# Feed-forward attention: the query side's band moves from four matmuls into VectorE's row maxima

## The chip, the cores and the metric

The kernel runs on one core of one Trainium2 chip. The metric is the time on the device in microseconds (us), the median of a few runs.

## The reference, cut to what matters

The program computes an adaptive-layernorm block: two attentions of 16 heads over four sequences of 1024 rows of 128, and then two layers of a feed-forward block that has a local attention of its own. The change touches that local attention alone:

```python
DIM_HEAD, WINDOW, HEADS = 64, 64, 8        # DEPTH = 2 layers
bq = q.reshape(b, h, w, WINDOW, d) * QK_SCALE          # 8.0
sim = jnp.einsum('bhwid,bhwjd->bhwij', bq, bk)         # keys: this window and the one before
mask = (i < j) | (i > j + WINDOW) | (j == -1)
sim = jnp.where(mask, -jnp.finfo(sim.dtype).max, sim)
attn = jax.nn.softmax(sim, axis=-1)
out = jnp.einsum('bhwij,bhwjd->bhwid', attn, bv)
```

A query at place i sees the keys from i - 64 to i. That is the band.

## The kernel before, in words

Rows are worked on in tiles of 128. The feed-forward half is one stream of 64 tiles (2 layers x 4 sequences x 8 tiles; `STREAM`), written as a software pipeline in `ffn_stream`: in period n each engine does some steps of tile n, some of n - 1, n - 2 and n - 3, in an order written out by hand in one loop for each engine. An engine runs its list strictly in order; semaphores hold an instruction until its operands are there. Besides, after every four tiles a chunk of 512 rows goes through the MLP (`CHUNK_TILES = 4`), and its steps are spread over the following periods by `step`, 0 to 3. So the pattern repeats every four periods. In this text the four are called A (step 0: `gate`, three `down` matmul pairs, `add_residual`, `finish`), B (step 1: `x_transposes`, `row_stats`), C (step 2: `normalise_rows`, first `up_gelu`) and D (step 3: the other `up_gelu`, three Gelus with two table loads).

The scores are computed twice. First on the query side, rows are queries: `query_scores(n)` (lines 1351 to 1371) makes q k^T in bf16 for 8 heads in two PSUM banks, 128 x 1024. From it comes the row maximum of every query and head (`row_maxima`, L1810), negated and in bf16. That is transposed (`max_transpose`, L1375), copied by ScalarE (`copy_max`, L1639) and added by small matmuls (L1393) to the second scores, `key_scores(n)` (L1387 to L1402), in which rows are keys. Their exponentials (L1646) feed `value_products` (L1416). A key outside a query's band must not enter its maximum, so the query side starts with four matmuls (L1359): a 64 x 64 corner of the bf16 identity times a band of 0 and -1e30, widened over four heads, written with `start=True`; the 16 score matmuls (L1367) are then added to it with `start=False`. The four corners (`CORNERS`) are the 64-row halves of both operands and of the output. The key side has a band of its own, L1387, which the change leaves alone.

For the first tile of a sequence there is no window before: `form = 1` is a band that hides the first 64 keys of queries 0 to 63, and their score matmuls write the upper 64 columns alone (`lo`).

TensorE's order in period n, around the change: project_qk(n) (L1327), project_v(n) (L1337), key_scores(n-2), qk_transposes(n-1) (L1347), value_products(n-2) (L1416), **query_scores(n-1)** (L1359, L1367), project_out(n-3) (L1438), MLP steps (L1463, L1448), out_transposes(n-2) (L1424), `down` in A (L1489), **max_transpose(n-1)** (L1375). That last one waits for `maxed`.

VectorE's order: normalise_rows in C (L1852), normalise_heads(n-1) (L1270), rope(n) (L1785, L1788), square_sums(n) (L1802, L1804), `gate` j=1 in A, norm_out(n-2) (L1819, L1824), `gate` j=2 in A (L1861), **row_maxima(n-1)** (L1810), gate j=0 in D, add_residual in A (L1836), row_stats in B (L1843, L1846), `finish` in A (L1869). norm_out waits for value_products; row_maxima waits for query_scores.

In the first six periods leftovers of the attention half (`tail_...`) run between these steps.

Of the kernel before, what the change touches and what calls it, by code (L numbers as in the profile page):

```python
# [23 lines left out]
BF16 = mybir.dt.bfloat16  # L24
ALU = mybir.AluOpType
ACT = mybir.ActivationFunctionType
AX = mybir.AxisListType.X

P = 128
B, S, D = 4, 1024, 128  # L30
TILES = S // P
BANK = 512
# [21 lines left out]
DEPTH, FH, FD = 2, 8, 64  # L54
INNER = FH * FD
WIN = 64
# [4 lines left out]
HIDDEN = -1e30  # L61
# [3 lines left out]
SIDES = 2  # L65
SIDE_HEADS = FH // SIDES
# [25 lines left out]
class Scope:  # L92
# [12 lines left out]
    def sb(self, name, shape, dtype=F32):  # L105
        return self.stack.enter_context(self.nc.sbuf_tensor(f"{self.prefix}_{name}", shape, dtype))
# [9 lines left out]
def widen(ap, shape):  # L116

    return ap.to_broadcast(shape)
# [1117 lines left out]
def ffn_stream(nc, psum, dram, keep, k, tail):  # L1236


    g = k.signals
    bank = lambda i, n=1: psum[:, i * BANK:(i + n) * BANK]  # L1240
    QK_BANK, V_BANK, SCORE_BANK, MAX_BANK, KEY_BANK, OT_BANK, WO_BANK, MLP_BANK = 0, 2, 2, 3, 4, 4, 6, 7
    UP_BANKS = {(0, 0): 7, (1, 0): 1, (2, 0): 0, (0, 1): 7, (1, 1): 7, (2, 1): 1}
    SIDE_ROWS = (slice(0, FD), slice(FD, P))
    CORNERS = ((0, 0), (1, 0), (0, 1), (1, 1))
# [12 lines left out]
    near, pick = stage[:, 0:P], stage[:, P:P + SIDE_HEADS * FD].rearrange("p (h c) -> p h c", h=SIDE_HEADS)  # L1257
# [14 lines left out]
    with nc.Block() as block:  # L1272
# [34 lines left out]
        def _(pe):  # L1307
            T = nc.tensor
# [42 lines left out]
            def query_scores(n):  # L1351
                t = n % TILES
                pe.wait_ge(g["qkt_copied"], n + 1)
                if n == 0:
                    pe.wait_ge(g["bands_ready"], 1)
                for side, block_n in CORNERS:
                    rows, c0 = SIDE_ROWS[side], (SCORE_BANK + side) * BANK
                    form = 1 if t == 0 and block_n == 0 else 0
                    T.matmul(psum[SIDE_ROWS[block_n], c0:c0 + BANK], keep.ident_bf[rows, rows],  # L1359
                             widen(k.band_bf[rows, form:form + 1, :], [FD, SIDE_HEADS, P]),  # L1360
                             start=True, stop=True)
                for i in range(SIDE_HEADS):
                    for side, block_n in CORNERS:
                        rows, q0 = SIDE_ROWS[side], t * P + block_n * WIN
                        lo = WIN if t == 0 and block_n == 0 else 0
                        c0 = (SCORE_BANK + side) * BANK + i * P
                        ins = T.matmul(psum[SIDE_ROWS[block_n], c0 + lo:c0 + P],  # L1367
                                       k.q_t_bf[rows, i, q0:q0 + WIN, 1],
                                       k.k_t_bf[rows, i, q0 - WIN + lo:q0 + WIN, 1],
                                       start=False, stop=True, skip_group_check=True)  # L1370
                ins.then_inc(g["s_in_psum"], 1)

            def max_transpose(n):
# [168 lines left out]
            for n in range(PERIODS):  # L1542
                c, step = divmod(n - 6, CHUNK_TILES)
# [180 lines left out]
        def _(pool):  # L1724
            steps = Chain(pool, g["pool_steps"])
            halves = lambda ap: ap.rearrange("p (h i d) -> p h i d", h=2 * FH, i=2)
            cleared = g["cleared"]
# [2 lines left out]
            pool.memset(k.max_t[:], 0.0).then_inc(cleared, 1)  # L1730
            pool.memset(k.neg_max[:], 0.0).then_inc(cleared, 1)
            pool.memset(k.xw[:, :, 0:1], 0.0).then_inc(cleared, 1)
            pool.memset(k.band_bf[:, 1, 0:WIN], HIDDEN).then_inc(cleared, 1)
            pool.memset(k.band_t_bf[:, 2, 0:WIN], HIDDEN).then_inc(cleared, 1)
            pool.memset(k.v_back[:], 0.0).then_inc(cleared, 1)
            gated_add(pool, steps, tail, keep, 2, g["tail_gated"])
# [31 lines left out]
        def _(dve):  # L1768
            steps = Chain(dve, g["dve_steps"])
            V = nc.vector  # L1770
# [35 lines left out]
            def row_maxima(n):  # L1806
                dve.wait_ge(g["s_in_psum"], n + 1)
                if n >= 2:
                    dve.wait_ge(g["mt_in_psum"], n - 1)
                steps.did(V.tensor_reduce(k.neg_max[:, n % 2, :].rearrange("p (s c) -> p s c", s=SIDES)[:, :, 0:SIDE_HEADS],  # L1810
                                          bank(SCORE_BANK, 2).rearrange("p (s i c) -> p s i c", s=SIDES, i=SIDE_HEADS),
                                          AX, ALU.max, negate=True), g["maxed"])

            def norm_out(n):
                dve.wait_ge(g["o_in_psum"], n + 1)
# [58 lines left out]
            def make_bands():  # L1874
                dve.wait_ge(g["loaded"], FIRST_LOADS)
                steps.did(V.tensor_copy(k.band_bf[:, 0, :], near))
                steps.did(V.tensor_copy(k.band_bf[:, 1, WIN:P], near[:, WIN:P]))
                steps.did(V.tensor_copy(k.band_t_bf[:, 0, :], near))
                steps.did(V.tensor_copy(k.band_t_bf[:, 1, 0:WIN], near[:, WIN:P]))
                steps.did(V.tensor_copy(k.band_t_bf[:, 1, WIN:P], near[:, 0:WIN]))  # L1880
                steps.did(V.tensor_copy(k.band_t_bf[:, 2, WIN:P], near[:, 0:WIN]))
                steps.did(V.tensor_copy(k.pick[:], pick), g["bands_ready"])
# [88 lines left out]
def ffn_half(nc, psum, dram, keep, tail):  # L1971
    with Scope(nc, "ffn", keep.stack) as k:
        sb = k.sb
# [17 lines left out]
        k.k_t_bf = k.k_t.bitcast(BF16).rearrange("p i (t w) -> p i t w", w=2)  # L1991
        k.v, k.v_back = sb("v", [P, RING, VF_COLS]), sb("v_back", [P, RING, VF_COLS])
        k.band_bf, k.band_t_bf = sb("band", [P, 2, P], BF16), sb("band_t", [P, 3, P], BF16)
        k.pick = sb("pick", [P, SIDE_HEADS, FD], BF16)
        k.neg_max, k.max_t = sb("neg_max", [P, 2, P], BF16), sb("max_t", [P, 2, P], BF16)
        k.probs = sb("probs", [P, 2, SIDES, SIDE_HEADS, P])
# [113 lines left out]
```

## Time and profile before

| what | value |
|---|---|
| median of 3 runs | 1262.74 us (1262.25 to 1264.91) |
| the profiled execution's own time | 1263.66 us |
| span in its profile | 1261.9 us |
| TensorE matmul busy | 1141.8 us, 90% |
| VectorE busy | 987.2 us, 78% |
| ScalarE busy | 830.2 us, 66% |
| GpSimd busy | 444.9 us, 35% |
| L1359, the query side's band | 256 matmuls of 64 x 512, 400 ns each |
| L1367, the query side's scores | 1024 matmuls, median 215 ns |
| L1810, the row maxima | 64 reductions of 128 x 1024, 77.6 us, 1213 ns each |

The feed-forward half begins at about 523 us. Matmuls are pipelined, and matmuls on different corners of the array run side by side, so durations of TensorE rows may not be added: what a group costs is read from when the next one starts. The same holds, by less, for VectorE: a row's duration reaches a little past the start of the next row.

### The profile page before, as it was taken

How to read it: one execution, taken by the hardware profiler on the slowest of the kernel's cores; microseconds unless marked ns; L12 is line 12 of the kernel's file. 1: busy time of each engine (PE TensorE's matmuls, PEld its weight loads, DVE VectorE, ACT ScalarE, POOL GpSimd, SP SyncE). 2: the span in 40 equal slices, each digit the busy share in tenths (PEclk: the TensorE clock that was granted, in tenths of full speed). 3: DMA queues.
4: the chain of work that ended last, by engine and by line, in shares of the span. 5: the costliest groups of instructions: out<-in, count | busy, mean ns of one | idle time of the engine just before them, and what ended most of it. 6: DMA issues, size and time to landing. Idle time of an engine off the chain costs nothing.

```text
span 1261.9 us, 36707 instructions
## 1 busy us (share of the span) xinstructions
PE 1141.8 (90%) x15602; PEld 693.7 (55%) x15602; DVE 987.2 (78%) x1556; ACT 830.2 (66%) x1229; POOL 444.9 (35%) x582
## 2 busy tenths in 40 slices
PE   4488889898989999778999999999999999999985
PEld 3133434344435655455666666676666666666662
DVE  7869685877768888896887887788778877887755
ACT  3498898989887867545556655665666566656541
POOL 2203221211206448855533433333333333333310
PEclk8599999999999989998999999999999999999997
DMA  3114120020213331100210110111111111111102
GB/s 106 34 25 137 50 91 35 18 101 18 69 51 135 119 134 69 50 18 20 82 24 22 30 30 16 26 30 24 24 27 23 28 23 27 28 23 28 27 6 67
DMA packets 37329, 59.78 MB, mean 47 GB/s; under 512 B 6416, under 2 KB 12464, under 8 KB 37168
## 3 DMA queue, kind: packets, MB, share of 16 engines
q1 hardware_dynamic: 35760, 56.61, 15.3%
q8 instruction: 124, 2.03, 0.7%
q10 hardware_dynamic: 1408, 0.84, 0.3%
q14 instruction: 37, 0.30, 0.1%
HBM read 22.58 MB, written 16.78 MB: 31 GB/s over the span
## 4 chain that ended last, share of the span: by engine, by line
PE 51%; DVE 4%; ACT 2%; issue 1%; DVEq 0%; ACTq 0%
PE psum L1327 9%; PE psum L1463 7%; PE psum L1416 6%; PE psum L1438 5%; PE psum L1402 5%; PE psum L1337 4%; PE psum L1347 4%; PE psum L1489 3%; PE psum L1424 2%; PE psum L1387 2%; PE psum L1359 2%; ACT ffn_probs L1646 2%; PE psum L1393 1%; PE psum L1367 1%; PE psum L1455 1%
## 5 line engine op out<-in xcount | busy, mean ns | idle before, releaser
L818 ACT ACTIVATE att_probs<-psum 128x1024 f32<-128x1024 f32 (+2 forms) x384 | 350.7, 988 | 44.5 <-PE psum L673 44.3
L1757 POOL TENSOR_TENSOR ffn_rot<-ffn_rot,ffn_rot_sin 128x512 f32<-128x512 f32 x128 | 160.2, 1273 | 372.5 <-DVE ffn_rot L1788 372.5
L717 PE MATMUL psum<-att_probs,att_v 128*32 128x256 f32 (+3 forms) x3712 | 201.4, 343 | 6.5 <-DVE att_probs L1010 3.2
L673 PE MATMUL psum<-att_q_stack,att_k_parts 64*128 64x512 bf16 (+4 forms) x1280 | 142.1, 296 | 41.8 <-ACT att_probs L818 30.4
L717 PEld LDWEIGHTS psum<-att_probs,att_v 128*32 128x32 f32 x3712 | 96.1, 110 | 72.0 <-issue 41.8
L1010 DVE TENSOR_TENSOR att_probs<-att_probs,att_causal_mask 128x1024 f32<-128x1024 f32 (+1 forms) x80 | 95.9, 1214 | 35.3 <-ACT att_probs L818 35.2
L673 PEld LDWEIGHTS psum<-att_q_stack,att_k_parts 64*128 64x128 bf16 x1280 | 43.5, 94 | 144.5 <-ACT att_probs L818 104.0
L1639 ACT ACTIVATE ffn_max_t<-psum 68x128 bf16<-68x128 bf16 x64 | 17.5, 273 | 156.8 <-PE psum L1375 156.7
L1646 ACT ACTIVATE ffn_probs<-psum 128x1024 f32<-128x1024 f32 x64 | 65.6, 1025 | 59.1 <-PE psum L1402 59.1
L1608 ACT ACTIVATE ffn_sq<-psum 128x512 f32<-128x512 f32 x128 | 74.7, 595 | 22.0 <-PE psum L1327 21.1
L604 POOL TENSOR_TENSOR att_rot<-att_qk 128x1280 f32<-128x1280 f32 x6 | 16.5, 2756 | 204.9 <-ACT att_qk L849 204.9
L1416 PEld LDWEIGHTS psum<-ffn_v_back,ffn_probs 128*64 128x64 f32 x1024 | 64.5, 137 | 31.8 <-ACT ffn_probs L1646 18.0
L585 POOL TENSOR_TENSOR att_probs<-att_probs,att_local_mask 128x480 f32<-128x480 f32 (+1 forms) x48 | 64.8, 1360 | 42.6 <-ACT att_probs L818 42.3
L1810 DVE TENSOR_REDUCE ffn_neg_max<-psum 128x8 bf16<-128x1024 f32 x64 | 77.6, 1213 | 0.0
L1802 DVE TENSOR_REDUCE ffn_ssq_floor<-ffn_sq 128x16 f32<-128x1024 f32 x64 | 77.3, 1208 | 0.0
L1416 PE MATMUL psum<-ffn_v_back,ffn_probs 128*64 128x65 f32 x1024 | 73.4, 224 | 2.1
L1270 DVE TENSOR_TENSOR ffn_rot<-ffn_rot,ffn_rnorm 128x704 f32<-128x704 f32 x64 | 68.9, 1077 | 7.9 <-POOL ffn_rnorm L129 7.3
L1347 PE MATMUL psum<-ident,ffn_rot 128*128 128x128 f32 x512 | 70.8, 282 | 3.3 <-DVE ffn_rot L1270 3.3
L1416 PE MATMUL psum<-ffn_v,ffn_probs 128*64 128x65 f32 x1024 | 73.4, 224 | 0.0
L1631 ACT ACTIVATE ffn_qk_t<-psum 128x1024 f32<-128x1024 f32 x64 | 65.6, 1025 | 10.4 <-PE psum L1347 10.4
L1402 PE MATMUL psum<-ffn_qk_t 64*64 64x64 f32 (+1 forms) x2944 | 70.1, 236 | 0.0
L1327 PE MATMUL psum<-tail_f_wqkv,xs 128*128 128x512 f32 x128 | 65.5, 637 | 3.2 <-PEq L539 1.8
(222 smaller groups left out, 2443.1 us busy)
## 6 DMA issues: line engine op xcount, KB each, us to landing
ffn_v_back<-ffn_v SPq DMA_DIRECT2D x120, 130.0 KB, 2.4
att_q_stack<-q_rows SPq DMA_DIRECT2D x28, 512.0 KB, 3.6
q_rows<-att_q_high SPq DMA_DIRECT2D x21, 256.0 KB, 4.5
q_rows<-att_q_mid SPq DMA_DIRECT2D x21, 256.0 KB, 4.2
q_rows<-att_q_low SPq DMA_DIRECT2D x14, 256.0 KB, 4.0
xres<-in_hidden SPq DMA_DIRECT2D x4, 512.0 KB, 6.1
out<-ffn_qk_t SPq DMA_DIRECT2D x3, 512.0 KB, 3.2
tail_f_wqkv<-in_f_wqkv SPq DMA_DIRECT2D x1, 768.0 KB, 4.5
```

Source lines behind the costliest of these rows:

```text
L673: ins = T.matmul(psum[:, banks[i] + at:banks[i] + at + width], k_parts[rows, p % 3, j, kt * P:(kt + 1) * P], q_stack[rows, turn % 2, j, q0 ...
L717: ins = T.matmul(psum[32 * g:32 * g + V_PAD, (4 + cc) * BANK + lo - cc * BANK: (4 + cc) * BANK + hi - cc * BANK], v[:, p % 4, kt, g, shift ...
L818: act.activation(probs[:, n % E_BUFS, 2 * j:2 * j + 2, 0:width], ps2((step % 2) * 2).rearrange("p (h c) -> p h c", h=2)[:, :, 0:width], AC ...
L1010: c.did(V.tensor_tensor(blocks, blocks, widen(seen, list(blocks.shape)), ALU.mult), masked)
L1327: T.matmul(bank(QK_BANK + i), keep.xs[:, b, t * P:(t + 1) * P], k.w_qkv[layer][:, i * INNER:(i + 1) * INNER], start=True, stop=True).then_ ...
L1347: ins = T.transpose(psum[:, SCORE_BANK * BANK + i * P:SCORE_BANK * BANK + (i + 1) * P], k.rot[:, n % 2, i * P:(i + 1) * P], keep.ident[:])
L1402: ins = T.matmul(psum[SIDE_ROWS[key_block % 2], c0 + lo:c0 + hi], k.k_t[rows, i, key_block * WIN:(key_block + 1) * WIN], k.q_t[rows, i, t ...
L1416: ins = T.matmul(psum[SIDE_ROWS[block_n], c0:c0 + VF], k.probs[:, n % 2, side, i, block_n * WIN:(block_n + 1) * WIN], values[:, n % RING, ...
L1463: T.matmul(psum[0:rows, UP_BANKS[j, part] * BANK:(UP_BANKS[j, part] + 1) * BANK], k.w1[layer][:, lo:lo + rows], k.hn[:], start=True, stop= ...
L1646: steps.did(act.activation(k.probs[:, n % 2].rearrange("p s i c -> p (s i c)"), bank(KEY_BANK, 2), ACT.Exp, scale=QK_SCALE), g["exped"])
L1757: steps.did(pool.tensor_tensor(out, out, halves(k.rot_sin[:, n % 2, :])[:, :, 1 - half, :], ALU.add), g["added"] if half else None)
L1810: steps.did(V.tensor_reduce(k.neg_max[:, n % 2, :].rearrange("p (s c) -> p s c", s=SIDES)[:, :, 0:SIDE_HEADS], bank(SCORE_BANK, 2).rearran ...
```

## The change

The four band matmuls go. The 16 score matmuls are written with `start=True`, and so hold plain scores. In place of one reduction over 8 heads VectorE runs, for each head, one fused operation: (scores + band) x -1 in bf16 to a new scratch tensor, and the minimum of it, from a start of 2e30, into that head's column of `neg_max`. The band is read from SBUF in bf16, now with all 128 query rows at once, so its second form is made for 128 rows too: the memset covers rows 0 to 63 and a cast more fills rows 64 to 127. The column of head i of side s is `64 s + i`, as before.

```diff
@@ query_scores(n), TensorE
-                for side, block_n in CORNERS:
-                    rows, c0 = SIDE_ROWS[side], (SCORE_BANK + side) * BANK
-                    form = 1 if t == 0 and block_n == 0 else 0
-                    T.matmul(psum[SIDE_ROWS[block_n], c0:c0 + BANK], keep.ident_bf[rows, rows],
-                             widen(k.band_bf[rows, form:form + 1, :], [FD, SIDE_HEADS, P]),
-                             start=True, stop=True)
...
-                                       start=False, stop=True, skip_group_check=True)
+                                       start=True, stop=True, skip_group_check=True)
@@ GpSimd, once
-            pool.memset(k.band_bf[:, 1, 0:WIN], HIDDEN).then_inc(cleared, 1)
+            pool.memset(k.band_bf[0:WIN, 1, 0:WIN], HIDDEN).then_inc(cleared, 1)
@@ row_maxima(n), VectorE
-                steps.did(V.tensor_reduce(k.neg_max[:, n % 2, :].rearrange("p (s c) -> p s c", s=SIDES)[:, :, 0:SIDE_HEADS],
-                                          bank(SCORE_BANK, 2).rearrange("p (s i c) -> p s i c", s=SIDES, i=SIDE_HEADS),
-                                          AX, ALU.max, negate=True), g["maxed"])
+                form = 0 if n % TILES else 1
+                for side in range(SIDES):
+                    for i in range(SIDE_HEADS):
+                        c0, column = (SCORE_BANK + side) * BANK + i * P, side * FD + i
+                        steps.did(V.tensor_tensor_reduce(k.hidden_scores[:, SIDE_HEADS * side + i], psum[:, c0:c0 + P], k.band_bf[:, form, :], -1.0,
+                                                         -2 * HIDDEN, ALU.add, ALU.min,
+                                                         k.neg_max[:, n % 2, column:column + 1]),
+                                  g["maxed"] if (side, i) == (SIDES - 1, SIDE_HEADS - 1) else None)
@@ make_bands(), VectorE, once
                 steps.did(V.tensor_copy(k.band_bf[:, 1, WIN:P], near[:, WIN:P]))
+                steps.did(V.tensor_copy(k.band_bf[WIN:P, 1, 0:WIN], near[WIN:P, 0:WIN]))
@@ ffn_half
+        k.hidden_scores = sb("hidden_scores", [P, FH, P], BF16)
```

What the diff does not show is what one call of `tensor_tensor_reduce` becomes in VectorE's queue. Here is that queue at a tile of kind B, before (`ffn_o` is the normalised attention output, `ffn_neg_max` the negated maxima, `ffn_stats` the MLP's row statistics):

```order
L1802 TENSOR_REDUCE ffn_ssq_floor<-ffn_sq 128x16 [waits ffn_rn_ready,ffn_sq_ready]
L1804 TENSOR_REDUCE ffn_ssq<-ffn_ssq_floor 128x16 [waits ffn_dve_steps]
L1819 RECIPROCAL ffn_o_rec<-psum 128x8 [waits ffn_o_in_psum]
L1824 TENSOR_TENSOR ffn_o<-psum,ffn_o_rec 128x2x4x64 [waits ffn_ot_in_psum,ffn_dve_steps]
L1810 TENSOR_REDUCE ffn_neg_max<-psum 128x2x4 [waits ffn_mt_in_psum,ffn_s_in_psum]
L1843 BN_STATS ffn_stats<-psum 128x6 [waits ffn_xt_in_psum]
```

And the head of the same place in the changed kernel, where the maxima have line 1808; the last two rows below come eight times in all, ahead of the row statistics:

```order
L1818 RECIPROCAL ffn_o_rec<-psum 128x8 [waits ffn_o_in_psum]
L1823 TENSOR_TENSOR ffn_o<-psum,ffn_o_rec 128x2x4x64 [waits ffn_ot_in_psum,ffn_dve_steps]
L1808 ISA ffn_hidden_scores,ffn_neg_max<-psum,ffn_band 128x128 [waits ffn_mt_in_psum,ffn_s_in_psum]
L1808 ISA ffn_neg_max 128x1
L1808 ISA ffn_hidden_scores,ffn_neg_max<-psum,ffn_band 128x128
L1808 ISA ffn_neg_max 128x1
```

Each call is two instructions: one over 128 x 128, and one of a single column that reads the running minimum out into `neg_max`. One instruction of 1024 columns has become sixteen, eight of 128 columns and eight of one. What stands ahead of them and behind them, and all waits, are the same. On TensorE the four rows of L1359 are gone and nothing has moved; the queues of ScalarE, GpSimd and SyncE hold the same instructions in the same order as before.

## Rows read from the trace of the kernel before

**Rows 1.** Busy time by stretch, feed-forward; the last columns are granted clock and DMA.

```profile
core 0: us, PE busy (x) PEld busy (x) DVE busy (x) ACT busy (x) POOL busy (x), PEclk, DMA share, GB/s
...
560.00:600.00 40.00, 33.29 (x473) 22.85 (x473) 29.13 (x57) 22.91 (x42) 24.25 (x28) 0.91 0.11 25
...
899.70:942.06 42.36, 42.25 (x616) 28.06 (x614) 34.12 (x52) 25.73 (x44) 16.20 (x28) 1.00 0.12 27
```

**Rows 2.** Timeline, VectorE: start us, us, engine, line, operation; the maxima of four tiles.

```profile
899.70 1.21 DVE L1810 TENSOR_REDUCE ffn_neg_max<-psum 128x8 bf16<-128x1024 f32 x1
...
909.38 1.21 DVE L1810 TENSOR_REDUCE ffn_neg_max<-psum 128x8 bf16<-128x1024 f32 x1
...
919.05 1.22 DVE L1810 TENSOR_REDUCE ffn_neg_max<-psum 128x8 bf16<-128x1024 f32 x1
...
929.62 1.22 DVE L1810 TENSOR_REDUCE ffn_neg_max<-psum 128x8 bf16<-128x1024 f32 x1
...
942.06 1.21 DVE L1810 TENSOR_REDUCE ffn_neg_max<-psum 128x8 bf16<-128x1024 f32 x1
```

**Rows 3.** Timeline, TensorE: the transposes of the maxima that follow them.

```profile
901.85 0.22 PE L1375 MATMUL psum<-ident_bf,ffn_neg_max 128*68 128x128 bf16 x1
...
910.85 0.22 PE L1375 MATMUL psum<-ident_bf,ffn_neg_max 128*68 128x128 bf16 x1
...
920.53 0.22 PE L1375 MATMUL psum<-ident_bf,ffn_neg_max 128*68 128x128 bf16 x1
...
931.52 0.22 PE L1375 MATMUL psum<-ident_bf,ffn_neg_max 128*68 128x128 bf16 x1
```

**Rows 4.** Timeline, TensorE: the band, the scores and what follows, one tile.

```profile
908.41 0.41 PE L1359 MATMUL psum<-ffn_band,ident_bf 64*64 64x512 bf16 x4
908.65 0.40 PE L1367 MATMUL psum<-ffn_qk_t 64*64 64x128 bf16 x16
908.98 1.16 PE L1438 MATMUL psum<-ffn_o_t,tail_space 128*128 128x128 f32 x8
```

**Rows 5.** Timeline, VectorE: from the maxima of A to those of B.

```profile
900.83 1.39 DVE L1836 TENSOR_TENSOR ffn_xw<-xs,psum 64x512 f32<-64x512 f32 x2
...
904.74 1.23 DVE L1785 TENSOR_TENSOR ffn_rot_sin<-psum,tail_space 128x1024 f32<-128x1024 f32 x1
...
908.53 0.21 DVE L1819 RECIPROCAL ffn_o_rec<-psum 128x8 f32<-128x8 f32 x1
908.77 0.69 DVE L1824 TENSOR_TENSOR ffn_o<-psum,ffn_o_rec 128x512 f32<-128x512 f32 x1
```

**Rows 6.** Timeline, VectorE: behind the maxima of B.

```profile
910.61 0.89 DVE L1843 BATCH_NORM_STATS2 ffn_stats<-psum 128x6 f32<-128x128 f32 x4
911.53 0.38 DVE L1846 BATCH_NORM_AGGREGATE ffn_mv<-ffn_stats 128x2 f32<-128x6 f32 x4
912.52 1.37 DVE L1852 TENSOR_SCALAR ffn_xn<-psum,ffn_mv,ffn_rstd 128x128 f32<-128x128 f32 x4 [0.60 <-ACT ffn_rstd L1661]
```

**Rows 7.** One line each, VectorE: duration ns min/median/max.

```profile
L1843 DVE BATCH_NORM_STATS2 ffn_stats<-psum x64: 278/281/300, 612.3 to 1235.1; 128x6 f32<-128x128 f32 x64
...
L1846 DVE BATCH_NORM_AGGREGATE ffn_mv<-ffn_stats x64: 147/151/184, 613.2 to 1235.7; 128x2 f32<-128x6 f32 x64
```

**Rows 8.** Timeline, VectorE: where it waits for TensorE, C to D and D to A.

```profile
928.77 0.21 DVE L1819 RECIPROCAL ffn_o_rec<-psum 128x8 f32<-128x8 f32 x1 [1.89 <-PE psum L1416]
...
941.39 0.75 DVE L1861 SCALAR_TENSOR_TENSOR tail_space<-psum,ffn_b,tail_space 85x512 f32<-85x512 f32 x1 [1.58 <-PE psum L1463]
```

**Rows 9.** Timeline: maxima that TensorE waited for, and the weight load behind them.

```profile
552.26 1.21 DVE L1810 TENSOR_REDUCE ffn_neg_max<-psum 128x8 bf16<-128x1024 f32 x1
...
553.53 0.11 PEld L1375 LDWEIGHTS psum<-ident_bf,ffn_neg_max 128*68 128x68 bf16 x1 [0.71 <-DVE ffn_neg_max L1810]
```

**Rows 10.** VectorE by line and form: two casts of the bands, the slowest and the fastest.

```profile
L1880 DVE CAST ffn_band_t<-ffn_probs 128x64 bf16<-128x64 f32 x1 | 1.3, 1289 | 0.0
...
L1877 DVE CAST ffn_band<-ffn_probs 128x64 bf16<-128x64 f32 x1 | 0.2, 202 | 0.0
```

## The prediction

> **What bounds the kernel now.** I read the busy time by stretch first. Over four tiles of the feed-forward stream, 42.36 us, TensorE's rows cover 42.25 us and VectorE's 34.12 us, at a granted clock of 1.00, its 2.4 GHz level [rows 1]. TensorE's cover says little, since its rows overlap; what counts is when each step starts. So next the timeline of the row maxima and of the transposes behind them. The maxima of the four tiles A, B, C, D start at 899.70, 909.38, 919.05 and 929.62, and the next A's at 942.06: distances of 9.68, 9.67, 10.57 and 12.44 us [rows 2]. These four numbers come back within 0.1 us from the start at 645.71 to the last A at 1196.05, so one round stands for all.
>
> Then, for each distance, what sets it. From A to B VectorE runs from one instruction into the next: none of its rows in that stretch shows idle time, and norm_out at 908.53 and 908.77 leads straight into B's maxima [rows 2, 5]. From B to C it idles 0.60 us, for ScalarE's two roots, which wait for its own row statistics [rows 6]; that gap moves along with the maxima. From C to D it waits 1.89 us for the value products, and from D to A 1.58 us for the MLP matmul ahead of gate L1861 [rows 8]: there TensorE sets the pace. The maxima are on TensorE's path as well: their transpose (L1375) is the last thing that it does in a period, and nothing of the next period can pass it. It starts 2.15 us after the start of A's maxima, 1.47 after B's, 1.48 after C's and 1.90 after D's [rows 2, 3]. A reduction takes 1.21 us, and where TensorE did wait for one, its weight load came 0.06 us after the end [rows 9]. So in B and C the transpose has some 0.2 us to spare, in D 0.6, in A 0.9.
>
> **What goes.** The next group starts 0.24 us after the four band matmuls do (908.41 to 908.65), though each row's duration is longer [rows 4]. So TensorE gets 0.24 us back per tile, 15 us over 64 tiles if nothing else held. It does not get it in A to B and B to C, where VectorE sets the distance. It gets it once ahead of L1861, and it brings D's transpose forward from 1.90 to 1.66.
>
> **What comes.** One reduction holds VectorE 1.13 us (899.70 to 900.83) and ends at 1.21 [rows 2, 5]. In its place stand sixteen instructions. No row shows a fused operation or a read-out of its result, so I bound a head by neighbours. Four statistics of 128 columns from PSUM take 0.89 us together, one of them 0.281: the next starts (0.89 - 0.281) / 3 = 0.203 us after the one before. Four aggregates of six columns take 0.38, one 0.151: a start every 0.076 us [rows 6, 7].
> - Low end, 0.203 us a head: the read-out is hidden behind the next head.
> - A start every 0.203 + 0.076 = **0.279** us a head. I take this: the two rows are instructions of the same engine, the same width and the same source, back to back without a wait, as the new ones are.
> - The read-out starts when the head's duration is over: 0.281 + 0.076 = 0.357.
> - High end, neither overlaps anything: 0.281 + 0.151 = 0.432.
>
> With 0.279 VectorE is held X = 8 x 0.279 = 2.23 us, and the last result is there at Z = X + 0.075 = 2.31, a read-out's duration reaching that far past its slot.
>
> The rows show that short independent instructions overlap. The Trainium skill, "VectorE: DVE Perf Modes", section "The DRAIN you can't avoid", says that the next operation cannot issue until the pipe is empty, and its rules for kernel authors say to minimise the count of operations; by that the high end would hold, 1397 us, a rival below. The same page, in "Two Vector instructions with no wait between them", counts an accumulator output as a second instruction that is held only for what it reads and where it writes; by that the read-out here is not held, and the value is the one that I take.
>
> **The sum, per round of four tiles.**
> - A to B, VectorE sets it: 2.23 - 1.13 = +1.10. TensorE's way would be Z + 0.10 to the transpose (0.06 from [rows 9] and up to some hundredths for the load), and 7.53 from there (901.85 to 909.38): 9.94, less than 9.68 + 1.10.
> - B to C, the same: +1.10. TensorE's way is 2.41 + 8.20 = 10.61 against 10.77.
> - C to D, TensorE sets it: the transpose comes at 2.41 in place of 1.48, and the 9.09 us from there to D's maxima stay: +0.93.
> - D to A: 2.41 in place of 1.90, less the band's 0.24 ahead of L1861: +0.27.
>
> That is **+3.40 us** a round; for a price d of a head it is 32 d - 5.53. Between the maxima at 602.23 and the last at 1214.60 lie 58 distances, 14.5 rounds: +49.3. The six tiles before are filled with leftovers of the attention half that stand in VectorE's queue behind the maxima: 6 x 1.10 = +6.6. The cast more in make_bands costs 0.2, and at worst 1.3 [rows 10]. The smaller memset and the scratch tensor cost nothing: they lie in GpSimd's idle time before the first scores and in free memory. The queues of ScalarE, GpSimd and SyncE hold what they held; their work moves with the tiles. Behind the longer maxima VectorE's queue holds A's residual, B's statistics, D's gate and then normalise_heads, for which TensorE's L1347 waits. VectorE's 8.2 us without a row in a round [rows 1] take this in C and D; in A and B it is the +1.10 already counted.
>
> Sum: 49.3 + 6.6 + 0.2 = +56 us. Against the profiled execution's 1263.66 that is 1319.8; the median of the runs lies 0.9 below that execution, so **1319 us**.
>
> **The rivals.**
> - *The read-out waits for its head*, 0.357 us. It needs the head's last element, which speaks for it. A round is +5.89: 14.5 x 5.89 + 6 x 1.73 + 0.2 = +96, 1359 us.
> - *Count of operations decides*, 0.432 us: 14.5 x 8.29 + 6 x 2.33 + 0.2 = +134, 1397 us. The starts in [rows 6] speak against it, as those are less than a duration apart.
> - *The read-out is hidden*, 0.203 us: 14.5 x 0.97 + 6 x 0.49 + 0.2 = +17, 1280 us. One more instruction in an in-order queue for nothing: the 0.076 of the aggregates speaks against it.
> - *Faster*: if eight heads cost no more than the one reduction, 0.141 us each, the maxima stay out of the way, and the band's matmuls come back twice in D to A and 0.17 in C to D: -0.65 a round, 14.5 x 0.65 = 9.4, 1253 us. It decides from d = 0.170 down, where 14.5 (32 d - 5.53) + 6 (8 d - 1.13) is zero. It would need instructions of 128 columns that start closer together than the 0.203 shown.
> - *The clock falls*: TensorE will stand still about 1 us in most tiles. From 560 to 600 us, where its rows cover 33.3 of 40 us, the granted clock was 0.91, between its levels of 1.2 and 2.4 GHz [rows 1]. At 0.91 the 19.4 us of a round that TensorE sets grow by 1.9: 14.5 x 1.9 = 28 on top, 1347 us. TensorE's cover after the change is some 42 of 46 us, nearer to the full clock's stretch.
>
> **How the numbers follow.** My forecast, with a head between 0.26 and 0.30 us (1309 to 1330 us), 50%; the read-out waits 24%; the read-out hidden 10%; count of operations 8%; clock 4%; faster 2%; no change, with d near 0.17, 2%. The range goes from the hidden read-out with a little below it, 1278, to the waiting read-out with some of a lower clock on top, 1372; left out are the count of operations, both small cases and the tails. A measurement of this kernel tells 0.2%, 2.5 us, from no change: faster 2%, same 2%, slower 96%.
>
> **What would show it.** In the profile of the changed kernel: sixteen VectorE rows for each tile, eight of them of one column, and from the first to the row behind them 2.2 us (2.9 if the read-out waits, 3.5 if the count decides). L1369, the transpose, waits for VectorE in nearly every tile, some 2.4 us after the maxima begin. Distances of maxima near 10.8, 10.8, 11.5 and 12.7 us. A granted clock of 1.00 from 650 to 1200 us. Time before 520 us unchanged. I am wrong if the distances of A to B and B to C grow by something else than the maxima do, or if those of C and D stay while the heads take over 2 us.

## The result: slower by 1.5%, a third of the forecast loss

| | before | after |
|---|---|---|
| median | 1262.72 us | 1282.03 us |
| ratio, with its 95% interval | | 1.0146 [1.0126, 1.0167] |
| span of the profiled execution | 1261.9 us | 1280.2 us |
| a round A to A, read from the maxima | 42.36 us | 43.37 us |

The time grew by 19.3 us where 56 were forecast. Of the four executions after, one took 1347.78 us at a mean granted clock of 0.831, the other three 1281.55 to 1282.07 us at 0.967 or 0.968, and everything below is of the latter kind. Lines of the page of the changed kernel: the span, the busy times and the chain of work that ended last, traced back from the last instruction.

```profile
span 1280.2 us, 37156 instructions
...
PE 1138.3 (89%) x15346; PEld 686.2 (54%) x15346; DVE 1017.2 (79%) x2517; ACT 830.4 (65%) x1229; POOL 443.6 (35%) x582
...
PE 27%; DVE 24%; issue 6%; ACT 2%; DVEq 0%; ACTq 0%
```

VectorE's rows cover 1017.2 us where they covered 987.2, TensorE's 1138.3 where it was 1141.8; ScalarE and GpSimd are within 1.3 us of before. In the chain VectorE has 24% of the span where it had 4%, TensorE 27% where it had 51%.

The groups by line and form of VectorE, after: output and input with their shapes, count, busy us, mean ns, idle time before:

```profile
L1808 DVE CUSTOM_DVE_ANT_0 ffn_hidden_scores<-psum,ffn_band 128x128 bf16<-128x128 f32 x512 | 112.4, 284 | 0.0
...
L1808 DVE DVE_READ_ACCUMULATOR2_ANT ffn_neg_max<- 128x1 bf16 x512 | 43.2, 84 | 0.0
```

The fused operation stands there as CUSTOM_DVE_ANT_0, its read-out as DVE_READ_ACCUMULATOR2_ANT, a row of its own that lasts 84 ns. Its duration says nothing yet of its price; the timeline does. VectorE from the maxima of one A to the next, after:

```profile
908.70 0.75 DVE L1860 SCALAR_TENSOR_TENSOR tail_space<-psum,ffn_b,tail_space 85x512 f32<-85x512 f32 x1 [1.36 <-PE psum L1457]
909.36 0.28 DVE L1808 CUSTOM_DVE_ANT_0 ffn_hidden_scores<-psum,ffn_band 128x128 bf16<-128x128 f32 x1
909.57 0.08 DVE L1808 DVE_READ_ACCUMULATOR2_ANT ffn_neg_max<- 128x1 bf16 x1
909.57 0.28 DVE L1808 CUSTOM_DVE_ANT_0 ffn_hidden_scores<-psum,ffn_band 128x128 bf16<-128x128 f32 x1
...
911.05 0.08 DVE L1808 DVE_READ_ACCUMULATOR2_ANT ffn_neg_max<- 128x1 bf16 x1
911.05 1.40 DVE L1835 TENSOR_TENSOR ffn_xw<-xs,psum 64x512 f32<-64x512 f32 x2
...
918.48 0.19 DVE L1798 TENSOR_REDUCE ffn_ssq<-ffn_ssq_floor 128x16 f32<-128x32 f32 x1
918.58 0.20 DVE L1818 RECIPROCAL ffn_o_rec<-psum 128x8 f32<-128x8 f32 x1
918.81 0.69 DVE L1823 TENSOR_TENSOR ffn_o<-psum,ffn_o_rec 128x512 f32<-128x512 f32 x1
919.42 0.28 DVE L1808 CUSTOM_DVE_ANT_0 ffn_hidden_scores<-psum,ffn_band 128x128 bf16<-128x128 f32 x1
...
929.54 0.28 DVE L1808 CUSTOM_DVE_ANT_0 ffn_hidden_scores<-psum,ffn_band 128x128 bf16<-128x128 f32 x1
...
940.52 0.28 DVE L1808 CUSTOM_DVE_ANT_0 ffn_hidden_scores<-psum,ffn_band 128x128 bf16<-128x128 f32 x1
...
952.73 0.28 DVE L1808 CUSTOM_DVE_ANT_0 ffn_hidden_scores<-psum,ffn_band 128x128 bf16<-128x128 f32 x1
```

The read-out of a head starts in the same moment as the next head (909.57 twice), and heads follow each other at 0.21 us. From the first head to the row behind them pass 1.69 us (909.36 to 911.05) where the reduction took 1.13 [rows 2, 5]. The forecast had 2.23. The distances of the maxima are 10.06, 10.12, 10.98 and 12.21 us; they were 9.68, 9.67, 10.57 and 12.44 [rows 2].

TensorE's transposes of the maxima in the same stretch, after, which answer to [rows 3]:

```profile
911.51 0.22 PE L1369 MATMUL psum<-ident_bf,ffn_neg_max 128*68 128x128 bf16 x1
...
921.24 0.24 PE L1369 MATMUL psum<-ident_bf,ffn_neg_max 128*68 128x128 bf16 x1 [0.78 <-DVE ffn_neg_max L1808]
...
931.36 0.24 PE L1369 MATMUL psum<-ident_bf,ffn_neg_max 128*68 128x128 bf16 x1 [0.31 <-DVE ffn_neg_max L1808]
...
942.35 0.24 PE L1369 MATMUL psum<-ident_bf,ffn_neg_max 128*68 128x128 bf16 x1
```

B's and C's transpose now wait for VectorE, 0.78 and 0.31 us of TensorE's own time; they come 1.82 us after the start of their maxima, where it was 1.47 and 1.48. D's comes 1.83 us after them where it was 1.90, so the maxima now hold it as well. A's comes after 2.15 as before. So the wait that the prediction named is there, and it is smaller.

### The profile page after: what moved, and what is told of

The parts are those of the page before. It is cut to its first block, busy times and chain, and to the rows that moved or that the text cites. A ratio compares the mean times of both kernels' runs of the same rounds, so it can differ in the third digit from the quotient of the medians.

```text
span 1280.2 us, 37156 instructions
## 1 busy us (share of the span) xinstructions
PE 1138.3 (89%) x15346; PEld 686.2 (54%) x15346; DVE 1017.2 (79%) x2517; ACT 830.4 (65%) x1229; POOL 443.6 (35%) x582
## 4 chain that ended last, share of the span: by engine, by line
PE 27%; DVE 24%; issue 6%; ACT 2%; DVEq 0%; ACTq 0%
DVE ffn_hidden_scores L1808 6%; PE psum L1457 6%; PE psum L1327 5%; PE psum L1410 3%; DVE ffn_ssq_floor L1796 3%; DVE ffn_rot L1782 3%; DVE ffn_rot_sin L1779 3%; PE psum L1432 3%; PE psum L1396 2%; PE psum L1347 2%; PE psum L1337 2%; DVE xs L1868 2%; DVE ffn_rot L1270 1%; DVE ffn_xn L1851 1%; DVE ffn_stats L1842 1%
## 5 line engine op out<-in xcount | busy, mean ns | idle before, releaser
L1808 DVE CUSTOM_DVE_ANT_0 ffn_hidden_scores<-psum,ffn_band 128x128 bf16<-128x128 f32 x512 | 112.4, 284 | 0.0
L1625 ACT ACTIVATE ffn_qk_t<-psum 128x1024 f32<-128x1024 f32 x64 | 65.5, 1024 | 10.0 <-PE psum L1347 10.0
```

What stands on the lines that cost most here:

```text
L1808: steps.did(V.tensor_tensor_reduce(k.hidden_scores[:, SIDE_HEADS * side + i], psum[:, c0:c0 + P], k.band_bf[:, form, :], -1.0, -2 * HIDDEN ...
```

## The experiments

My theory after the result: a further instruction costs VectorE a fixed piece and the read-out nothing; the removed band pays only where VectorE is not the one waited for. In the table a round is the sum of the four distances, read from each run's timeline of VectorE. D to A alternates by 0.06 to 0.08 from round to round (12.37 and 12.44 before); the longer one is given, and both where they differ by 0.16.

| kernel | median us | ratio to before | A to B | B to C | C to D | D to A | round |
|---|---|---|---|---|---|---|---|
| before | 1262.7 | | 9.68 | 9.67 | 10.57 | 12.44 | 42.36 |
| after | 1282.03 | 1.0146 | 10.06 | 10.12 | 10.98 | 12.21 | 43.37 |
| bands kept, heads fused | 1284.24 | 1.0169 | 10.06 | 10.12 | 10.99 | 12.43 | 43.60 |
| bands gone, one reduction | 1254.52 | 0.9935 | 9.68 | 9.56 | 10.43 | 12.00, 12.16 | 41.75 |
| no read-out | 1275.12 | 1.0096 | 9.95 | 10.01 | 10.88 | 12.10 | 42.94 |
| eight plain reductions | 1277.57 | 1.0119 | 9.95 | 10.01 | 10.88 | 12.43 | 43.27 |
| four plain reductions | 1267.60 | 1.0038 | 9.69 | 9.76 | 10.63 | 12.43 | 42.51 |
| after, pair ahead of the scores | 1278.52 | 1.0121 | 11.12 | 10.12 | 10.99 | 10.93 | 43.16 |
| after, pair behind the scores | 1275.30 | 1.0100 | 10.57 | 10.12 | 10.99 | 11.28 | 42.96 |
| after, less scaling | 1277.36 | 1.0118 | 9.93 | 10.00 | 10.99 | 12.21 | 43.13 |
| before, less scaling | 1261.21 | 0.9991 | 9.68 | 9.55 | 10.70 | 12.43 | 42.36 |
| before, pair behind the scores | 1263.01 | 1.0002 | 10.57 | 9.67 | 10.58 | 11.51 | 42.33 |
| fused in A alone, pair behind the scores | 1259.62 | 0.9976 | 10.57 | 9.67 | 10.58 | 11.29 | 42.11 |

**VectorE's half alone.**

```diff
@@ the changed kernel
+                for side, block_n in CORNERS:
+                    rows, c0 = SIDE_ROWS[side], (SCORE_BANK + side) * BANK
+                    form = 1 if t == 0 and block_n == 0 else 0
+                    T.matmul(psum[SIDE_ROWS[block_n], c0:c0 + BANK], keep.ident_bf[rows, rows],
+                             widen(k.band_bf[rows, form:form + 1, :], [FD, SIDE_HEADS, P]),
+                             start=True, stop=True)
...
-                                       start=True, stop=True, skip_group_check=True)
+                                       start=False, stop=True, skip_group_check=True)
```

> The changed kernel, with the four band matmuls put back ahead of the scores (so hidden scores get the band twice, which does not alter a maximum). Only VectorE's half of the change is left. Theory (one head's fused operation costs one instruction slot of 0.21 us, its read-out nothing; the band's removal pays only where VectorE is not the one waited for): the distances of the maxima stay 10.06, 10.12 and 10.98 us, and the one from D to A goes from 12.21 to 12.45, so +0.24 a round, 14.5 rounds, +3.5: 1285.5 us. Rival (the removal pays 0.24 us in each of 64 tiles and the heads cost more than that): +15, 1297 us.

Measured: 1284.24 us, 1.0169 [1.0154, 1.0184]. Only D to A moved, by 0.22. The band's removal is worth 2.2 us inside the change by the medians (3.1 by the 58 distances between the maxima of the two traces), where the rival had 15.

**TensorE's half alone.**

```diff
@@ the kernel before
-                for side, block_n in CORNERS:
+                for side, block_n in CORNERS if t == 0 else ():
...
-                                       start=False, stop=True, skip_group_check=True)
+                                       start=t > 0, stop=True, skip_group_check=True)
...
-                                         ACT.Exp, scale=QK_SCALE), g["exped"])
+                                         ACT.Exp, scale=QK_SCALE / 64), g["exped"])
```

> The kernel before, with the band matmuls left out in all tiles but the first of each sequence, and one plain reduction as before: TensorE's half of the change alone. The query side's maxima then count hidden keys too, and the exponentials' scale is 1/64 of what it was so that sums stay above zero; neither alters a duration. Theory: A to B unchanged, B to C 0.10 shorter (the transposes ahead of the row statistics come earlier), C to D 0.11 shorter, D to A 0.24 shorter by A's own band and 0.24 more in every second round by D's: -0.57 a round, -8 us, 1254 us. Rival (each tile gets its 0.24 back): 56 x 0.24 = -13, 1249 us. Rival (hidden anyway): 1262.7.

Measured: 1254.52 us, 0.9935 [0.9919, 0.9952], with distances as expected within 0.05. So the same four matmuls, here taken out of 56 of the 64 tiles, are worth 8.2 us while the maxima are short and 2.2 when they are long. By the distances it is 7.9 us, without one place in tile 7 that is told under "Less work on VectorE", against 3.1. The fused maxima cover 60 to 75% of what the removal frees.

**The read-out taken away.**

```diff
@@ the changed kernel
-                                                         -2 * HIDDEN, ALU.add, ALU.min,
-                                                         k.neg_max[:, n % 2, column:column + 1]),
+                                                         -2 * HIDDEN, ALU.add, ALU.min, None),
```

> The changed kernel without the eight read-outs of a tile: the fused operations run as before, but their minima are never written, so the maxima stay zero. Theory (the read-out runs beside the next head): a head still starts every 0.21 us and the time stays within 1 us of the changed kernel, 1281 to 1283. Rival (the read-out costs the few ns by which 0.211 is over the 0.203 of the statistics): heads every 0.203, 8 x 0.008 x 64 = 4 us at most, 1278. Rival of the prediction (0.076 each): 8 x 0.076 less a tile would be -39 us.

Measured: 1275.12 us, 1.0096 [1.008, 1.0111], 6.9 less than the change. My theory of a free read-out falls, and so do both sizes of the rivals. VectorE in that run, the eight heads of a tile and the row behind them:

```profile
905.78 1.66 DVE L1808 CUSTOM_DVE_ANT_0 ffn_hidden_scores<-psum,ffn_band 128x128 bf16<-128x128 f32 x8
907.36 1.39 DVE L1834 TENSOR_TENSOR ffn_xw<-xs,psum 64x512 f32<-64x512 f32 x2
```

Eight heads take 1.58 us, 0.197 each, against 1.69 with their read-outs: a read-out costs 0.11 / 8 = 0.013 us, though it starts beside the next head. All four distances are 0.10 to 0.12 shorter, so 14.5 x 0.43 = 6.2 of the 6.9 us are in the rounds.

**Eight plain reductions.**

```diff
@@ the kernel before, row_maxima
-                steps.did(V.tensor_reduce(k.neg_max[:, n % 2, :].rearrange("p (s c) -> p s c", s=SIDES)[:, :, 0:SIDE_HEADS],
-                                          bank(SCORE_BANK, 2).rearrange("p (s i c) -> p s i c", s=SIDES, i=SIDE_HEADS),
-                                          AX, ALU.max, negate=True), g["maxed"])
+                for side in range(SIDES):
+                    for i in range(0, SIDE_HEADS, 1):
+                        c0, column = (SCORE_BANK + side) * BANK + i * P, side * FD + i
+                        steps.did(V.tensor_reduce(k.neg_max[:, n % 2, column:column + 1],
+                                                  psum[:, c0:c0 + 1 * P].rearrange("p (i c) -> p i c", c=P),
+                                                  AX, ALU.max, negate=True),
+                                  g["maxed"] if (side, i) == (SIDES - 1, SIDE_HEADS - 1) else None)
```

> The kernel before, bands and all, with the one reduction of 128 x 1024 split into eight plain reductions of 128 x 128. Theory (what costs is the fixed 0.07 to 0.08 us of each further instruction on VectorE, not the fused form): a reduction starts every 0.21 us, 1.68 in place of 1.13, and the time is that of the fused form with bands kept, 1285 us. Rival (the fused form itself is slow, plain ones are not): 1263 to 1268 us.

Measured: 1277.57 us, 1.0119 [1.0104, 1.0134]. Its maxima and the row behind them:

```profile
906.83 1.66 DVE L1813 TENSOR_REDUCE ffn_neg_max<-psum 128x1 bf16<-128x128 f32 x8
908.41 1.39 DVE L1840 TENSOR_TENSOR ffn_xw<-xs,psum 64x512 f32<-64x512 f32 x2
```

Again 1.58 us, where the expectation had 1.68, and so 7 us less than it said. A plain reduction of 128 columns and a fused operation without its read-out cost the same: the fused form is not slow. Splitting alone makes +14.9 us; the read-outs on top +6.7 (1284.24 - 1277.57, both with bands); the band's removal -2.2. These three make the 19.3 of the change.

**Four plain reductions.** Two heads each, against the kernel with eight:

```diff
-                    for i in range(0, SIDE_HEADS, 1):
+                    for i in range(0, SIDE_HEADS, 2):
...
-                        steps.did(V.tensor_reduce(k.neg_max[:, n % 2, column:column + 1],
-                                                  psum[:, c0:c0 + 1 * P].rearrange("p (i c) -> p i c", c=P),
+                        steps.did(V.tensor_reduce(k.neg_max[:, n % 2, column:column + 2],
+                                                  psum[:, c0:c0 + 2 * P].rearrange("p (i c) -> p i c", c=P),
...
-                                  g["maxed"] if (side, i) == (SIDES - 1, SIDE_HEADS - 1) else None)
+                                  g["maxed"] if (side, i) == (SIDES - 1, SIDE_HEADS - 2) else None)
```

> The kernel before with its reduction split into four of 128 x 256, two heads each. Theory (every further instruction holds VectorE some 0.064 us longer, and the first 0.1 to 0.2 us a tile are swallowed by gaps that the profile does not mark: 0.17 from A to B, 0.10 from B to C, 0.1 ahead of C's transpose): 1.32 us in place of 1.13, distances 9.70, 9.76, 10.60 and 12.44, 1265 us. Rival (the loss goes by the count of instructions: three sevenths of the 14.9 us that eight of them cost): 1269 us.

```profile
899.94 1.40 DVE L1813 TENSOR_REDUCE ffn_neg_max<-psum 128x2 bf16<-128x256 f32 x4
901.26 1.39 DVE L1840 TENSOR_TENSOR ffn_xw<-xs,psum 64x512 f32<-64x512 f32 x2
```

They take 1.32 us (899.94 to 901.26), as expected: one instruction 1.13, four 1.32, eight 1.58, so 0.064 us for each further one. The distances are those expected within 0.03 in the round of the table, and 0.06 in later ones (C to D 10.66), and the profiled execution is 1265.56 us. The median of the runs, 1267.6, 1.0038 [1.0028, 1.0048], lies 2 us above it and between the two expectations. Two microseconds are a head start: the profiled execution reached its first maxima at 538.97 us, the one of before at 540.99, though the kernels are the same up to there. From the first maxima on it is 3.9 us longer than before, 2.7 of them in the 58 distances. The total doesn't tell the two expectations apart; how the first instructions' loss is swallowed is settled by the distances alone.

**Who sets A to B.** In the changed kernel the matmuls ahead of A's gate went in front of the query scores.

```diff
@@ TensorE's loop
+                if step == 0 and live_chunk(c - 1):
+                    up_gated(c - 1, 2, n)
                 if live(n - 1):
                     query_scores(n - 1)
...
-                if step == 0 and live_chunk(c - 1):
-                    up_gated(c - 1, 2, n)
```

> The changed kernel with one MLP matmul pair (the last up_gated, ahead of the gate that A's maxima wait behind) moved in front of the query scores on TensorE. Theory (from A to B VectorE alone sets the distance, and TensorE could do it in 0.38 us less): A's maxima start over 1 us earlier, from A's transpose on TensorE sets the pace, B to C and C to D stay: a round is 0.38 shorter, 5.5 us, 1276.5 us. Rival (the 0.38 comes from TensorE's own path): no change, 1282.

Measured: 1278.52 us, 1.0121 [1.01, 1.0142]. VectorE from A's gate to B's maxima:

```profile
906.58 0.75 DVE L1860 SCALAR_TENSOR_TENSOR tail_space<-psum,ffn_b,tail_space 85x512 f32<-85x512 f32 x1
907.24 0.28 DVE L1808 CUSTOM_DVE_ANT_0 ffn_hidden_scores<-psum,ffn_band 128x128 bf16<-128x128 f32 x1
...
911.04 1.53 DVE L1868 SCALAR_TENSOR_TENSOR xs<-psum,ffn_vec,ffn_xw 64x512 f32<-64x512 f32 x2 [0.72 <-PE psum L1483]
...
917.51 0.21 DVE L1818 RECIPROCAL ffn_o_rec<-psum 128x8 f32<-128x8 f32 x1 [0.29 <-PE psum L1410]
...
918.37 0.28 DVE L1808 CUSTOM_DVE_ANT_0 ffn_hidden_scores<-psum,ffn_band 128x128 bf16<-128x128 f32 x1
```

A's maxima start 1.3 us earlier (D to A 10.93 in place of 12.21), and VectorE now waits, 0.72 us for the last `down` and 0.29 for B's value products: TensorE sets the distance. D to A and A to B together fell from 22.27 to 22.05, 0.22 where 0.38 was expected. TensorE around the moved pair:

```profile
905.45 1.09 PE L1457 MATMUL psum<-ffn_hn,ffn_w 128*85 128x512 f32 x2
906.47 0.43 PE L1361 MATMUL psum<-ffn_qk_t 64*64 64x128 bf16 x16
```

The scores start 1.02 us after the pair. In the changed kernel, where the pair is in its old place, the transposes behind it start 0.86 after it:

```profile
907.63 1.02 PE L1457 MATMUL psum<-ffn_hn,ffn_w 128*85 128x512 f32 x2
908.49 0.60 PE L1418 MATMUL psum<-ident,ffn_o 128*128 128x128 f32 x4
```

That is 0.16, just what is missing. The next run puts the pair behind the scores:

```diff
@@ TensorE's loop, the changed kernel
                 if live(n - 1):
                     query_scores(n - 1)
+                if step == 0 and live_chunk(c - 1):
+                    up_gated(c - 1, 2, n)
...
-                if step == 0 and live_chunk(c - 1):
-                    up_gated(c - 1, 2, n)
```

> The changed kernel with the same MLP pair moved only one step forward, behind the query scores and ahead of the output projection. Theory (the earlier place lost 0.16 us because a bf16 group stood right behind a fp32 group of 512 columns; the VectorE bound from A to B is real): D to A and A to B together 0.38 shorter, 14.5 x 0.38 = 5.5, 1276.5 us. Rival (no more than the 0.22 of the first place is to be had): 1278.5.

Measured: 1275.3 us, 1.01 [1.0085, 1.0115]. D to A and A to B together are 21.85, 0.42 shorter: the VectorE bound from A to B was real, and the place of the pair cost the 0.16 to 0.2.

**Less work on VectorE.** Two more heads' scaling goes to GpSimd:

```diff
-DVE_NORM = 11
+DVE_NORM = 9
```

In the changed kernel:

> The changed kernel with two more of the 16 head scalings (L1270) on GpSimd: DVE_NORM 9 in place of 11, so VectorE's instruction has 128 columns less, 0.133 us. Theory (VectorE sets A to B and B to C, TensorE the other two): both of the first get 0.13 shorter, 14.5 x 0.27 = 3.9, 1278 us. Rival (VectorE sets all four): 7.7 us, 1274. Rival (GpSimd becomes late for the transposes): slower than 1282.

Measured: 1277.36 us, 1.0118 [1.0099, 1.0137]: A to B and B to C 0.13 and 0.12 shorter, the others unmoved. In the kernel before:

> The same step in the kernel before, DVE_NORM 9. Theory (before the change A to B ends with TensorE, 0.17 us behind VectorE, and only B to C is VectorE's): B to C 0.13 shorter, 14.5 x 0.13 = 1.9, 1260.8 us. Rival (as the prediction had it, both are VectorE's): 3.9, 1258.8. Rival (GpSimd becomes late): slower than 1262.7.

Measured: 1261.21 us, 0.9991 [0.998, 1.0001]. The time is near the expected one, but not on its grounds. The maxima of one round in that run, from A to A:

```profile
896.74 1.21 DVE L1810 TENSOR_REDUCE ffn_neg_max<-psum 128x8 bf16<-128x1024 f32 x1
...
906.42 1.22 DVE L1810 TENSOR_REDUCE ffn_neg_max<-psum 128x8 bf16<-128x1024 f32 x1
...
915.97 1.21 DVE L1810 TENSOR_REDUCE ffn_neg_max<-psum 128x8 bf16<-128x1024 f32 x1
...
926.67 1.21 DVE L1810 TENSOR_REDUCE ffn_neg_max<-psum 128x8 bf16<-128x1024 f32 x1
...
939.10 1.21 DVE L1810 TENSOR_REDUCE ffn_neg_max<-psum 128x8 bf16<-128x1024 f32 x1
```

A to B is unmoved at 9.68, as expected. B to C is 0.12 shorter, and C to D 0.13 longer: a round is what it was. C's transpose stands behind TensorE's own work, so earlier maxima only wait longer for it. I had missed that. Before the change nearly the whole round is TensorE's.

What made the run shorter stands in one place, the scaling of tile 7. VectorE and GpSimd there, before:

```profile
615.52 3.03 DVE L1270 TENSOR_TENSOR ffn_rot<-ffn_rot,ffn_rnorm 128x704 f32<-128x704 f32 x1
...
615.44 2.36 POOL L1229 TENSOR_TENSOR tail_space<-tail_base_cos,tail_f_scales 128x1024 f32<-128x1024 f32 x1
```

And in this run:

```profile
614.54 0.80 DVE L1270 TENSOR_TENSOR ffn_rot<-ffn_rot,ffn_rnorm 128x576 f32<-128x576 f32 x1
...
614.68 2.89 POOL L1229 TENSOR_TENSOR tail_space<-tail_base_cos,tail_f_scales 128x1024 f32<-128x1024 f32 x1
```

Before, VectorE's scaling started 0.08 us behind GpSimd's product and took 3.03 us, where its median is 0.89. Here it started 0.14 us ahead, took 0.80, and GpSimd's took 0.5 us more. This one distance is 11.82 us before and 9.59 here; the other 57 add up to the same within 0.13 us. The run without bands has the short form too (9.56), and in the traces of all other kernels VectorE's instruction comes second and takes 2.57 to 3.03 us.

**A version that beats both.** Fused maxima only in A, with the pair behind the scores:

```diff
@@ the kernel before
+    fused = lambda n: n >= 5 and n % 4 == 1
...
-                for side, block_n in CORNERS:
+                for side, block_n in () if fused(n) else CORNERS:
...
-                                       start=False, stop=True, skip_group_check=True)
+                                       start=fused(n), stop=True, skip_group_check=True)
...
-                steps.did(V.tensor_reduce(k.neg_max[:, n % 2, :].rearrange("p (s c) -> p s c", s=SIDES)[:, :, 0:SIDE_HEADS],
-                                          bank(SCORE_BANK, 2).rearrange("p (s i c) -> p s i c", s=SIDES, i=SIDE_HEADS),
-                                          AX, ALU.max, negate=True), g["maxed"])
+                if fused(n):
+                    form = 0 if n % TILES else 1
+                    for side in range(SIDES):
+                        for i in range(SIDE_HEADS):
+                            c0, column = (SCORE_BANK + side) * BANK + i * P, side * FD + i
+                            steps.did(V.tensor_tensor_reduce(k.hidden_scores[:, SIDE_HEADS * side + i], psum[:, c0:c0 + P], k.band_bf[:, form, :], -1.0,
+                                                             -2 * HIDDEN, ALU.add, ALU.min,
+                                                             k.neg_max[:, n % 2, column:column + 1]),
+                                      g["maxed"] if (side, i) == (SIDES - 1, SIDE_HEADS - 1) else None)
+                else:
+                    steps.did(V.tensor_reduce(k.neg_max[:, n % 2, :].rearrange("p (s c) -> p s c", s=SIDES)[:, :, 0:SIDE_HEADS],
+                                              bank(SCORE_BANK, 2).rearrange("p (s i c) -> p s i c", s=SIDES, i=SIDE_HEADS),
+                                              AX, ALU.max, negate=True), g["maxed"])
```

> A hybrid: the kernel before, but with the fused maxima and no band matmuls in the tiles of kind A alone (15 of 64), and the MLP pair moved behind the query scores. Theory (with the gate early, TensorE and not VectorE sets A to B, so the eight instructions cost nothing there, and TensorE gets A's 0.24 us back ahead of A's transpose): 14.5 x 0.24 = 3.5 shorter, 1259 us, faster than both. Rival (VectorE still sets A to B): 14.5 x (0.38 - 0.24) = 2 longer, 1265.

> The control for the hybrid: the kernel before with the MLP pair moved and nothing else. Theory (before the change A to B ends with TensorE): no change, 1262.7 within 1 us. Rival (the hybrid's gain comes from the moved pair): 1259.

Measured: the hybrid 1259.62 us, 0.9976 [0.9966, 0.9986]; the control 1263.01 us, 1.0002 [0.9991, 1.0013]. The hybrid's VectorE, one round:

```profile
895.67 0.75 DVE L1872 SCALAR_TENSOR_TENSOR tail_space<-psum,ffn_b,tail_space 85x512 f32<-85x512 f32 x1 [0.43 <-PE psum L1464]
896.34 0.28 DVE L1816 CUSTOM_DVE_ANT_0 ffn_hidden_scores<-psum,ffn_band 128x128 bf16<-128x128 f32 x1
...
899.58 1.53 DVE L1880 SCALAR_TENSOR_TENSOR xs<-psum,ffn_vec,ffn_xw 64x512 f32<-64x512 f32 x2 [0.16 <-PE psum L1490]
...
906.06 0.21 DVE L1830 RECIPROCAL ffn_o_rec<-psum 128x8 f32<-128x8 f32 x1 [0.29 <-PE psum L1417]
...
906.91 1.21 DVE L1821 TENSOR_REDUCE ffn_neg_max<-psum 128x8 bf16<-128x1024 f32 x1
...
916.59 1.22 DVE L1821 TENSOR_REDUCE ffn_neg_max<-psum 128x8 bf16<-128x1024 f32 x1
...
927.16 1.21 DVE L1821 TENSOR_REDUCE ffn_neg_max<-psum 128x8 bf16<-128x1024 f32 x1
...
938.45 0.28 DVE L1816 CUSTOM_DVE_ANT_0 ffn_hidden_scores<-psum,ffn_band 128x128 bf16<-128x128 f32 x1
```

Behind the eight heads VectorE waits for `down` (0.16) and for the value products (0.29): their 0.56 us more fall into a gap that the moved pair has made, and TensorE keeps the band's 0.24. The round is 42.11 us against 42.36.

## Why the prediction was right in direction and wrong in size

The step that failed is the price of a head, "a start every 0.203 + 0.076 = 0.279 us a head". Measured is 0.211: 0.197 for the head and 0.013 for its read-out. With the size of the price right, the sum would have given 1284 us and not 1319. I had taken the read-out for one more short instruction like the aggregates, and it ran beside the next head. The rival with a hidden read-out, given 10% and 1280 us, had the mechanism right but for 0.013 us. That its time came within 2 us is in part luck: its 0.203 is 0.008 under the measured price, which is 4 us in its sum, and the gaps named below take most of that back.

Point by point, for a round:

| distance | forecast | measured |
|---|---|---|
| A to B | +1.10 | +0.38 |
| B to C | +1.10 | +0.45 |
| C to D | +0.93 | +0.41 |
| D to A | +0.27 | -0.23 |
| round | +3.40 | +1.01 |

With 0.211 put into 32 d - 5.53 the same steps give +1.22. A to B and B to C grew by 0.29 less than that, C to D and D to A by 0.07 more. Two waits explain the 0.29 within 0.02; neither is marked as idle in the profile of before. From A to B the reciprocal at 908.53 [rows 5] came 0.27 us after this small reduction; in the changed kernel, where VectorE is late, 0.10 (918.48 to 918.58):

```profile
908.26 0.19 DVE L1804 TENSOR_REDUCE ffn_ssq<-ffn_ssq_floor 128x16 f32<-128x32 f32 x1
```

So A to B ended with TensorE by 0.17 us, and "none of its rows in that stretch shows idle time" was true and not enough. In B the statistics started 1.23 us after the maxima [rows 2, 6], where the reduction holds VectorE 1.13: another 0.10 of waiting. For the first speak the four reductions and the lesser scaling in the kernel before: 0.19 us more left A to B at 9.69, 0.13 less left it at 9.68. For the second speaks the run without bands, whose B to C is 0.11 shorter. Part of the 0.07 more comes where the transpose had to wait: the next group then starts 0.10 or 0.11 us behind it (942.35 to 942.45, 931.36 to 931.47) and not 0.05; no run tests that by itself.

- *"In D to A the band's 0.24 ahead of L1861"*: right, 0.22 in the run with bands kept.
- *The first six tiles, "6 x 1.10 = +6.6"*: from the first maxima to those of the sixth tile, five distances, the time grew by 2.4 us (63.64 against 61.24); with 0.56 a tile it would have been 2.8. These five scatter: the three other kernels that keep the one reduction in these tiles and all bands have 60.2 to 63.4 us.
- *The cast, 0.2*: not to be seen. The first maxima start 0.28 us later, but their start lies between 538.97 and 541.64 us over all kernels, and with the same cast in the run with bands kept it is 540.99, as before.
- *Rounds*: 58 distances grew by 15.1 us, where 49.3 were forecast, and 0.56 came after the last maxima. 0.28 + 2.40 + 15.1 + 0.56 = 18.3, the difference of the spans.
- *The clock*: the granted clock was 1.00 from 650 to 1200 us, with TensorE's rows covering 42.17 of 43.37 us in the round shown. In the executions compared here that rival is out.
- *Count of operations decides* (the Trainium skill, "VectorE: DVE Perf Modes", section "The DRAIN you can't avoid"): out. Heads start 0.21 us apart and last 0.284. For operations that are not held that section points to the page's "Two Vector instructions with no wait between them", by which a read-out is not held, and this agrees with 909.57 twice.
- *Faster from d = 0.170 down*: not reached. The run without bands, 1254.5, has 0.61 us a round of the 0.65 that were calculated; that its total is so near 1253 is partly the 2.3 us of tile 7.

## What to carry to other kernels

Fusing a step into the reduction is paid by the instruction: one reduction over eight heads became eight, and 7 x 0.064 us of fixed time a tile and 8 x 0.013 for the read-outs cost more than the four matmuls gave. Before adding work to an engine, compare the gap between two of its rows with the same gap elsewhere in the trace: two waits of 0.17 and 0.10 us carried no mark here, and they decided who set the pace. A fused step belongs into those periods in which its engine waits anyway: here the same step gained 3 us in A alone, once the pair had been moved. And a total can be near an expectation for a reason of its own, as tile 7 showed; compare the distances before you believe it.

## What the runs showed of the hardware that I had not expected

- The read-out of a fused operation's result starts together with the next operation and costs it 0.013 us, against a row duration of 0.084.
- Reductions of 1024, 256 and 128 columns hold VectorE 1.13, 0.33 and 0.197 us: 0.064 us each beside their columns. The Trainium skill, "Vector Engine (DVE) Microarchitecture Reference", section "Measured stream behaviour on trn2", has about 75 ns; here it is less.
- The bf16 scores on 64-row corners, right behind the fp32 pair of 512 columns, start 1.02 us after it; the fp32 transposes start 0.86 after it, the fp32 output projection 0.93. Whether the type or the corners cost it, no run separates.
- A VectorE product of two SBUF tensors that starts just behind a GpSimd product lasts until after that one's end (3.03 us in place of 0.89); where it starts first, GpSimd's takes 0.5 to 0.7 us more (2.36 against 2.89 and 3.09).
